# Two diffusion tiles moved into the later groups of the first step, and the closing normalisation given its own buffers and early loads

## The reference, cut to what matters

```python
Xf, Xa = X, X
for s in range(2):
    logits = (Xa @ W1) @ W2 @ (Xa @ W3).T
    A = softmax(logits, keeping per row the largest until they hold 0.9)
    Xf = R @ Xf                     # "diffusion"
    Xa = A @ Xa
    Z = Z + Xf @ U1s[s] + Xa @ U2s[s]
out = x + layernorm(X + Z) * gamma + beta
```

## Time and profile before

| | |
|---|---|
| median of three runs | 1296.33 us (1292.09 to 1300.24) |
| the profiled execution, its own time | 1295.24 us |
| its span | 1293.3 us |
| mean granted TensorE clock | 0.953 |
| busy: PE, DVE, ACT, POOL | 1119.5, 1035.7, 439.4, 281.2 us |

### The profile page before, as it was taken

One profiled execution on the slowest core, in us unless ns is written; L12 is line 12 of the kernel. 1 busy time (PEld: TensorE's weight loads), 2 busy tenths in 40 slices (PEclk: granted clock), 3 DMA queues, 4 the chain that ended last, 5 costly groups with the idle time before them and its releaser, 6 DMA issues.

```text
span 1293.3 us, 16644 instructions
## 1 busy us (share of the span) xinstructions
PE 1119.5 (87%) x5402; PEld 518.1 (40%) x5402; DVE 1035.7 (80%) x2202; ACT 439.4 (34%) x836; POOL 281.2 (22%) x252
## 2 busy tenths in 40 slices
PE   0567999998999799799997999898999799789764
PEld 0223445454434344344443444343444344334321
DVE  7987777773599998899698006998997999999965
ACT  2544344444633033533432237540241251100000
POOL 6133333333122200101112010421111021011012
PEclk9888999999999899899998999898999899899887
DMA  7126466453334542341732513236844552743595
GB/s 244 65 69 220 166 205 209 168 199 118 95 117 153 143 89 43 90 82 42 147 82 66 96 51 130 90 117 243 193 91 136 134 115 90 187 114 107 148 266 156
DMA packets 190115, 170.62 MB, mean 132 GB/s; under 512 B 144656, under 2 KB 144656, under 8 KB 185936
## 3 DMA queue, kind: packets, MB, share of 16 engines
q1 hardware_dynamic: 190032, 169.66, 46.7%
HBM read 87.31 MB, written 48.76 MB: 105 GB/s over the span
## 4 chain that ended last, share of the span: by engine, by line
DVE 34%; PE 27%; issue 20%; POOL 7%; DMA 5%; ACT 5%; SPq 1%; POOLq 1%; DVEq 1%; ACTq 0%
PE RB L937 5%; DVE WS L1490 5%; DVE cand L1708 4%; PE UB L775 4%; PE AB L937 4%; DVE E L1721 3%; PE XB L775 3%; DVE WS L1705 3%; DVE WS L1713 3%; PE RB L939 3%; DVE g L1570 2%; PE AB L939 2%; DMA AD<-xu_d 2%; DVE E L1461 2%; DVE E L1720 2%
## 5 line engine op out<-in xcount | busy, mean ns | idle before, releaser
L1570 DVE TENSOR_REDUCE g<-E 128x1 f32<-128x2048 f32 x32 | 73.0, 2281 | 100.3 <-ACT E L1160 100.0
L1490 DVE SCALAR_TENSOR_TENSOR WS<-E,g 128x2048 bf16<-128x2048 f32 x48 | 119.6, 2535 | 0.4
L655 POOL TENSOR_TENSOR RT<-RT,AD 128x512 f32<-128x512 f32 x32 | 56.5, 1765 | 289.3 <-ACT RT L1220 289.2
L1708 DVE MAX8 cand<-WS 128x8 f32<-128x128 f32 x512 | 102.1, 276 | 1.1
L937 PE MATMUL AB<-VR,turns 128*128 128x512 f16 x256 | 66.3, 406 | 27.7 <-DMA turns<-E 27.7
L1713 DVE SCALAR_TENSOR_TENSOR WS<-E,g 128x2048 f32<-128x2048 f32 x33 | 80.9, 2450 | 0.9
L937 PE MATMUL RB<-VR,turns 128*128 128x512 f16 x256 | 64.2, 396 | 19.5 <-DMA turns<-E 19.5
L1721 DVE SCALAR_TENSOR_TENSOR E<-WS,E 128x2048 f16<-128x2048 f32 x32 | 79.1, 2472 | 1.1
L937 PE MATMUL RB<-XR,turns 128*128 128x512 f16 x256 | 63.8, 394 | 17.9 <-DMA turns<-E 17.9
L1197 ACT ACTIVATE E<-E,nmx 128x2048 f32<-128x2048 f32 x32 | 63.7, 1993 | 42.9 <-DVE nmx L1571 42.9
L672 POOL TENSOR_TENSOR XHL<-WF,XHL 128x512 f16<-128x512 f32 x16 | 22.1, 1383 | 250.0 <-ACT XHL L1245 250.0
(11 more groups left out here) (316 smaller groups left out, 2210.0 us busy)
## 6 DMA issues: line engine op xcount, KB each, us to landing
turns<-adj_parts SPq DMA_DIRECT2D x48, 512.0 KB, 3.8
E<-adjT SPq DMA_DIRECT2D x16, 1024.0 KB, 7.6
adj_parts<-turns SPq DMA_DIRECT2D x16, 1024.0 KB, 5.2
AH<-adj_parts SPq DMA_DIRECT2D x16, 512.0 KB, 4.1
z_d<-UO SPq DMA_DIRECT2D x28, 256.0 KB, 2.3
XR<-x SPq DMA_DIRECT2D x4, 1024.0 KB, 11.8
WS<-U SPq DMA_DIRECT2D x4, 1024.0 KB, 7.5
x_d<-WF SPq DMA_DIRECT2D x16, 256.0 KB, 2.0
```

What stands on the lines that cost most here:

```text
L1490: return v.scalar_tensor_tensor(junk[t % 2], e, g4[:, k, t:t + 1], e, op, ALU.mult, accum_out=g4[:, F_, t:t + 1])
L1570: ct(v.tensor_reduce(row(A2)[:, t:t + 1], E[:, slot, :], AX.X, ALU.max))
L1708: i = v.max(cand[:, t, 8 * c:8 * c + 8], WS[:, c * PART:(c + 1) * PART])
```

## The change

`R_BEHIND` becomes ((0, 1, 1, 1), (1, 3, 4, 3)) and `R_LATE` 4: groups 1, 2 and 3 of the first step have one diffusion tile each (9, 10, 11); the second step's head has four late tiles (12 to 15) and five of its own (0 to 4), nine as before; its groups 1 and 3 have three instead of four. The logits of the second step's group 1 now follow the woven late tile at once.

The closing part: the y of batches 0, 1, 2 have E slots 0, 1, 2; their x1 the memory of UW and UV (free once the first step is over) and E slot 3; the last group's x1 goes into the memory of XR's first tiles. x1 of batches 0 and 1 and gamma are loaded at the start of the second step's group 2; the rest at the start of group 3, ahead of its diffusion tiles, y of batch 2 after the first of them. The last tiles end in four buffers. In the last group `z_in(t + 1)` comes after the transposes of tile t + 1, and all outputs are issued after the last `z_in`.

```diff
-R_LATE = 6
-R_BEHIND = ((0, 0, 1, 0), (1, 4, 4, 4))
+R_LATE = 4
+R_BEHIND = ((0, 1, 1, 1), (1, 3, 4, 3))
...
-        fin_y = [E[:, 2 * h, :].rearrange("p (t d) -> p t d", t=G) for h in range(2)]
-        fin_x = [E[:, 2 * h + 1, :].rearrange("p (t d) -> p t d", t=G) for h in range(2)]
+        fin_y = [E[:, b, :] for b in range(NG - 1)]
+        fin_x = [u[:, :, :, :].rearrange("p k h d -> p (k h d)").bitcast(F32) for u in (UW, UV)] + [E[:, NG - 1, :]]
...
-        gam, ends = WF, (UO, XF)
-        end_x = WS[:, :].rearrange("p (t d) -> p t d", t=G)
+        gam, ends = WF, (UO, XF, RT, AD)
...
+                if s == 1 and g == 2:
+                    sp.wait_ge(s_wl, T)
+                    fin_x_in(0)
+                    fin_x_in(1)
+                    sp.wait_ge(s_gb, 16)
+                    sp.dma_start(gam[:, :], gamma.partition_broadcast(P)).then_inc(s_gb, 16)
+                if s == 1 and g == NG - 1:
+                    for c in range(NC):
+                        sp.wait_ge(s_et[c], 16 * (T + G * (NG - 1)))
+                    fin_y_in(0)
+                    fin_y_in(1)
+                    fin_x_in(2)
                 rows = diffusion(s, g)
-                for rs, t in rows[:-1]:
+                for j, (rs, t) in enumerate(rows[:-1]):
                     r_done(rs, t, t % 2)
+                    if s == 1 and g == NG - 1 and j == 0:
+                        fin_y_in(2)
...
-                    if s:
+                    if s and (i == 0 or not last):
                         z_in(t)
...
                     if last and i == 0:
+                        sp.wait_ge(s_r, 2 * T)
                         end_in()
-                        fin_out(0, 1)
-                    if last and i == 1:
-                        fin_in(2)
-                        fin_out(1, 2)
-                    if last and i == 2:
-                        end_out(T - G, 3)
-                        fin_out(2, 4)
-                    if last and i == 3:
-                        end_out(T - G + 1, 5)
+                    if last and i < G - 1:
+                        z_in(t + 1)
+                if last:
+                    fin_out(0, 1)
+                    fin_out(1, 2)
+                    end_out(T - G, 3)
+                    fin_out(2, 4)
+                    for k in range(1, G):
+                        end_out(T - G + k, 4 + k)
```

More of the change, by code:

```diff
@@ L179, in build @@
         BATCHES = NG - 1
-        fin_y = [E[:, 2 * h, :].rearrange("p (t d) -> p t d", t=G) for h in range(2)]
-        fin_x = [E[:, 2 * h + 1, :].rearrange("p (t d) -> p t d", t=G) for h in range(2)]
+        fin_y = [E[:, b, :] for b in range(NG - 1)]
+        fin_x = [u[:, :, :, :].rearrange("p k h d -> p (k h d)").bitcast(F32) for u in (UW, UV)] + [E[:, NG - 1, :]]
+        fin_y, fin_x = ([u.rearrange("p (t d) -> p t d", t=G) for u in us] for us in (fin_y, fin_x))
+        end_x = XR[:, 0:G, :, :].rearrange("p t h d -> p t (h d)").bitcast(F32)
         mean_w = PKf
         bet, X1B = XHL[:, :, :].rearrange("p h d -> p (h d)").bitcast(F32), WF
-        gam, ends = WF, (UO, XF)
-        end_x = WS[:, :].rearrange("p (t d) -> p t d", t=G)
+        gam, ends = WF, (UO, XF, RT, AD)
         def halves_of(slot):
@@ L248, in build @@
             "s_zin", "s_y", "s_yout", "s_fvar", "s_frs", "s_res", "s_out")]
-        s_finx, s_finy, s_end = ([sem(f"{n}{h}") for h in range(2)] for n in ("s_finx", "s_finy", "s_end"))
-        s_endx = sem("s_endx")
+        s_finx, s_finy = ([sem(f"{n}{b}") for b in range(NG - 1)] for n in ("s_finx", "s_finy"))
+        s_endx, s_end = sem("s_endx"), sem("s_end")
         s_xin = [sem(f"s_xin{b}") for b in range(NG)]
@@ L276, in step_order @@
                 r_one(0, T - R_LATE)
-                r_span(0, T - R_LATE + 1, T - 3)
+                if R_LATE > 4:
+                    r_span(0, T - R_LATE + 1, T - 3)
                 logits(s, 1)
@@ L440, in z0_store, with fin_x_in, fin_y_in @@
                 sp.dma_start(z0_d[t], UO[:, :]).then_inc(s_uout, 16)
[L442 to L447, removed]
+            def fin_x_in(b):
+                sp.dma_start(fin_x[b], x1_d[G * b:G * b + G].rearrange("t p d -> p t d")).then_inc(s_finx[b], 16)
+            def fin_y_in(b):
                 sp.wait_ge(s_yout, 16 * (G * b + G) + OPEN)
-                sp.dma_start(fin_y[b % 2], z1_d[rows].rearrange("t p d -> p t d")).then_inc(s_finy[b % 2], 16)
+                sp.dma_start(fin_y[b], z1_d[G * b:G * b + G].rearrange("t p d -> p t d")).then_inc(s_finy[b], 16)
             def fin_out(b, nth):
                 sp.wait_ge(s_res, nth)
-                if b:
-                    sp.wait_ge(s_out, 16 * b)
-                sp.dma_start(out[G * b:G * b + G].rearrange("t p d -> p t d"), fin_y[b % 2]).then_inc(s_out, 16)
+                sp.dma_start(out[G * b:G * b + G].rearrange("t p d -> p t d"), fin_y[b]).then_inc(s_out, 16)
             def end_in():
-                sp.wait_ge(s_kept, 2 * T)
                 sp.dma_start(end_x, x1_d[T - G:T].rearrange("t p d -> p t d")).then_inc(s_endx, 16)
@@ L462, in end_out @@
                 sp.wait_ge(s_res, nth)
-                sp.dma_start(out[t], ends[t % 2][:, :]).then_inc(s_end[t % 2], 16)
+                sp.dma_start(out[t], ends[t % G][:, :]).then_inc(s_end, 16)
             def stores(t):
@@ L490, in pairs @@
                 last = s == 1 and g == NG - 1
[L491 to L498, removed]
                 for i in range(G):
@@ L548, in _ @@
             step_order(1, nothing, nothing, r_one, r_span, group_start, pairs, last_post)
-            end_out(T - G + 2, 6)
-            end_out(T - G + 3, 7)
             sp.wait_ge(s_rout, 16 * T + OPEN)
             sp.wait_ge(s_out, 16 * BATCHES)
-            for h in range(2):
-                sp.wait_ge(s_end[h], 16 * (G // 2))
+            sp.wait_ge(s_end, 16 * G)
         @block.gpsimd
@@ L694, in pairs @@
                         root(0, 0, G)
-                    y = ends[t % 2] if g == NG - 1 else UO
+                    y = ends[t % G] if g == NG - 1 else UO
                     pool.wait_ge(s_zin, 16 * t + 16)
@@ L1257, in a_out @@
                     if t >= T - G + 2:
-                        act.wait_ge(s_end[t % 2], 16)
-                    y = ends[t % 2] if t >= T - G else UO
+                        act.wait_ge(s_rout, 16 * T + OPEN)
+                    y = ends[t % G] if t >= T - G else UO
                     a(y[:, :], bank[:, :], ACT.Copy, scale=rden[:, slot:slot + 1]).then_inc(s_ue, 1)
@@ L1851, in batch @@
             def batch(b, nth):
-                dve.wait_ge(s_finx[b % 2], 16 * (b // 2) + 16)
-                dve.wait_ge(s_finy[b % 2], 16 * (b // 2) + 16)
-                normed([(G * b + t, fin_y[b % 2][:, t, :], fin_x[b % 2][:, t, :]) for t in range(G)], nth)
+                dve.wait_ge(s_finx[b], 16)
+                dve.wait_ge(s_finy[b], 16)
+                normed([(G * b + t, fin_y[b][:, t, :], fin_x[b][:, t, :]) for t in range(G)], nth)
             def end(t, nth):
                 dve.wait_ge(s_y, t + 1 + OPEN)
-                normed([(t, ends[t % 2][:, :], end_x[:, t - (T - G), :])], nth)
+                normed([(t, ends[t % G][:, :], end_x[:, t - (T - G), :])], nth)
             dve.wait_ge(s_gb, 32)
```

## The result

The changed kernel takes **1287.63 us** (median of six runs, 1284.95 to 1290.3), the kernel before 1295.95 beside it: a ratio of 0.9933, 95% interval 0.991 to 0.9956. The forecast was 1285 in a range of 1278 to 1296. The profiled execution took 1287.91 us with a span of 1286.1, 7.2 us less than before.

The account below looks back on a forecast made before the run. Bound: PE in the first step, DVE in the second to the last mask, then DVE's wait for batch 2's y. 1295.24 + 3.0 - 3.5 - 10.8 = 1283.9 us profiled, 1.09 under the median: 1285, range 1278 to 1296.

Parts of the forecast that it names:

- The first step's two added tiles: Starts of groups 1 and 3: tiles fill PE's wait for SP's stores, together +3.0 us, bounds 0 and 20.7.
- Group 3's term: First step, group 3's start: its added tile brings it to group 2's stretch, 31.12 us from 28.38, costing 2.7 us.
- the 33 us that were to show me wrong: Sign of error: first-step group starts, first carried matmul to second tile's first, stretching beyond 33 us.
- The second step's head on DVE: Group 0's search: only two POOL operations remain beside DVE instead of six, -3.5 us, bounds 0 and -5.
- The head on PE: Second step's start: PE reaches group 0's first turned tile 20.7 us later, but DVE does not wait; 0 us.
- Rival (a): Second step: DVE starves for group 2's logits, PE lagging 29.3 us against 25.1; 4 us wait, 1289 us, chance 0.10.
- Loads ahead of groups 2 and 3: Second step: bulk loads hold a diffusion tile 4 to 7 us once each, covered by PE's wait at group 3.
- The end: After the last mask: batch 2's y in its own slot removes DVE's wait, moving all behind it by -10.83 us.
- (b): First step: the two added tiles cost their full 20.7 us, since PE sets a group's start; 1303 us, chance 0.08.
- (c): Closing part: outputs bunch at 9.7 us each and tile 15's output lands behind them; 1297 us, chance 0.07.
- (d): Closing part: batch 2 waits as before, for its y or a root held by POOL's order; 1296 us, chance 0.08.
- (e): Closing part gives more: no gaps at tiles 13 and 14, no slow matmuls or stretched operations; 1281 us, chance 0.12.

Follow-up runs that it names:

- load late: Changed kernel with y of batch 2 loaded in the last group behind z of tile 13, not between group 3's diffusion tiles: 1288.69 us.
- order alone: Kernel before with only the change's new constants (order of the diffusion tiles), old closing part: 1297.18 us, ratio 1.0013.
- sums first: Changed kernel with GpSimd taking the last tiles' sums ahead of the roots it used to wait for: 1276.33 us.
- end alone: Changed kernel with the old constants (order of tiles of the kernel before), so only the closing part is new: 1286.7 us, ratio 0.9935.
- transposes first: Changed kernel with SP issuing a group's first transposes before storing the carried tile, in the first step's groups 1, 2, 3: 1282.16 us.
- third tile in group 0: Changed kernel with its third first-step diffusion tile ahead of group 0 instead of group 3: 1283.18 us, ratio 0.9911.

## Why the prediction came out as it did

**The number.** 1287.63 us for 1285, a gain of 8.3 us for 11.3. The range, 1278 to 1296, also held "no gain at all", so lying in it proves little. Against the profiled execution, 1287.91 for 1283.9, the terms missed by +3.0 us (first step), +1.6 (second) and -0.4 (end): nothing large was cancelled by luck, and the closing part made the whole gain.

**What bounds.** Right in all three stretches: what the first step lost showed in full at the second step's first maximum, what the head lost on PE showed nowhere, and the last mask set the end.

**The first step's two added tiles, +3.0 us.** The mechanism was right, the size was not: the stores gate the group, and a tile put there costs little. Group 1's term held (+0.3 said, -0.07 measured). Group 3's term of **+2.7 us**, taken from group 2, is the term that was mis-sized: in the changed kernel's profile it was +5.8, and with 34.14 us the stretch passed the 33 us that were to show me wrong. Three more profiles with the same first step gave 30.04, 30.55 and 34.09 against 28.38 without a tile, so it is 1.7 to 5.8 us and falls into two kinds: with a wait of 1.83 or 2.70 us PE goes on at its usual pace, with 3.56 or 3.77 it restarts at the lower clock. What decides is where POOL's L673 falls against DVE's mask: in all four L673 starts 13.1 us after the group's first carried matmul, and the mask starts 0.11 us ahead of it in the changed kernel, 0.32 in load late and 1.65 in order alone, so that L673 takes 3.26, 3.05 and 1.72 us (with sums first it meets another instruction and takes 2.10). The same instruction also holds group 2 (2.81 us at 618.99, wait 2.95 for 1.53), whose price, +1.0 to +2.0 us, I had put at nothing.

**The second step's head on DVE, -3.5 us.** Measured -2.6 us for the search and -1.9 us to the last mask. The mechanism was right: over all twelve profiles that search takes 31.1 us with six operations of POOL in it, 29.4 with four and 28.4 to 28.5 with three, and group 1's 27.5 to 27.6 with two; each costs DVE some 0.9 us. My count was wrong. I had said that only the woven tile's two operations would fall there; a third one does, of the next late tile (836.58). And the operations are moved as much as removed: group 1's search now has three and takes 28.60 us for 27.58.

**The order as a whole** was put at -0.5 us and is +1 by two pairs of kernels, with an interval of 0 to 3.5 us. With this order first maxima lie from 787.40 to 791.81 in four profiles, without it at 783.85 and 784.87; the second step gives back 2 us, and order alone's closing part was 1.3 us shorter.

**The head on PE, 0.** Held: no wait of DVE, and 5.9 us of slack left where 4.4, or 0.6 with the slow restart, were said. The stall at (1,0) is 14.31 us for 14, the one at the logits of group 1 longer by 8.0 us (11.87 for 3.92) where 10 was said. That PE came at 940.27 for the 937 said is partly chance: the whole step began 5.99 us later, and from its first maximum PE is 17.8 us later, not 20.7. The slow restart did happen, but cost about 1.8 us and not 3.8 (1.03 and 5.00 us, where 0.61 and 3.62 are usual). Rival (a) stays below its point.

**Loads ahead of groups 2 and 3, 0.** Nothing in DVE's second step shows them: in end alone, which has these loads and the old order, it takes 447.01 us from the first maximum to the last mask, for 446.76. PE's wait for group 3's first turned tile is 19.38 us in the changed kernel, where 18.5 of cover was said.

**The end, -10.83.** -11.25 by the profile, 9.4 us by the medians of end alone, whose interval (5.6 to 11.3 us) holds both. Z of tile 14 went out at 1262.00, 27.3 us after the last mask (27 was said). What I hadn't asked is which part of the edit was needed: load late shows that the buffer alone was. Nor did I ask what was late next beyond PE's tile 14: POOL's order held tile 13's sum behind batch 2's root, and that was worth 10 us more.

**Rivals.** (b), two tiles at full price, fell for this kernel, and its point of decision was nearly right: with the wait gone they cost 8.5 us each, not 10.36. (c) fell: the three large outputs were issued from 1269.02 to 1271.31, and tile 15's output at 1283.57 ended the span 2.5 us later. (d) and (e) fell.

## What to carry to other kernels

A wait that an added piece of work fills hides its price: before filling it, ask what it waits for, since removing it (here one store moved behind four transposes, 19.2 us) may be worth more than the work placed in it, and turns that work into cost. After a wait is taken from the end, follow each queue for the next one that stands behind the same event. A price read from one group of one profile should be read from several, above all where it ends near a wait that may or may not restart PE at its lower clock.

## What the runs showed of the hardware

**POOL and DVE take turns.** L673 takes 1.16 us alone (530.69 in the changed kernel). In four profiles that of group 3 started beside DVE's mask, at different places of it, and ended 1.02 us after the mask's end: 705.57 and 706.59 in the changed kernel; 705.68 and 706.70 in order alone, 707.38 and 708.40 in load late, 704.38 and 705.40 in transposes first. With sums first it met DVE's L1725 (end 703.95) and ended at 704.96, 1.01 us later. DVE pays as well: in the changed kernel its next instruction took 2.06 us instead of 1.23. The Trainium skill (SBUF — State Buffer, Who interferes with whom) says that a DVE instruction with two SBUF inputs contends with a GpSimd one that reads SBUF, and that so does one in a two-port mode, where the later of the two "fully blocks". The trace agrees: the mask, `scalar_tensor_tensor(WS, E, ..., E)`, reads two, and the 1.02 us behind it are close to the 1.16 us that L673 takes alone. No run here was made to tell the number of inputs from the mode as the reason.

**The lower clock is not a matter of the wait alone.** At the group starts of the first step waits of 1.83 and 2.95 to 3.00 us left eight matmuls at 1.89 us, one of 3.13 gave 2.33, and 3.56 and more gave 2.99 to 3.57 (the 1.2 GHz level for most or all of the eight). But the same wait of 2.10 us was followed by 1.89 with the third tile in group 0 (537.69) and by 2.96 in transposes first (635.28), and the carried product at 773.10 ran at 4.13 us for twelve behind waits of 1.21 and 0.78 us, with a granted clock of 0.89 from 769 to 784, where the changed kernel has the same two waits and 2.75 us. The Trainium skill (TensorE: Matmul & The Clock Gate, Part 1: The HAM clock gate) calls the number of slow matmuls at a kernel's start "run-variable". These rows, of restarts inside a kernel, agree: some 1.7 us can come or go at such a place behind a wait of the same length. What decides it stays open.
